# Attention in a decoder block: v's two halves in one product, their sums added once a batch

## The reference

```python
x = x + attn(layernorm(x), w_qkv, w_proj)      # 16 heads of 32, causal softmax, 1.58-bit linear layers
x = x + xattn(layernorm(x), k, skip, ctx, ctx) # long convolution of v*x2 along 512, weighed by x1
x = x + ffn(layernorm(x), gate, up, down, scales)  # silu(gate) * up, weights rounded to fp8
```

```python
attn = einsum('bnhd,bmhd->bhnm', q, k) * SCALE   # masked, then softmax over m
out = einsum('bhnm,bmhd->bnhd', softmax(attn), v).reshape(B, N, C)
return bitlinear(out, w_proj)                    # rounds rows of out by their maximum
```

## Time and profile before

| | us |
|---|---|
| median of 3 runs | 1649.04 (1647.38 to 1649.38) |
| profiled execution | 1647.97 |
| its span | 1646.2 |
| PE busy | 1517.4 (92%) |
| DVE busy | 1280.9 (78%) |
| POOL busy | 974.4 (59%) |
| ACT busy | 676.7 (41%) |
| mean granted TensorE clock | 0.979 |

### The profile page before, as it was taken

How to read it: one execution, slowest core, us unless ns; L and a number is a source line. 1 busy time by engine, 2 the same in 40 slices (tenths; PEclk the granted TensorE clock), 3 DMA queues, 4 the chain that set the end, 5 groups by cost and what they waited for, 6 DMA issues and landing times.

```text
span 1646.2 us, 27188 instructions
## 1 busy us (share of the span) xinstructions
PE 1517.4 (92%) x10581; PEld 869.8 (53%) x10581; DVE 1280.9 (78%) x1865; ACT 676.7 (41%) x1214; POOL 974.4 (59%) x706
## 2 busy tenths in 40 slices
PE   2589999999996778899999999999999999999998
PEld 2477787878774333444444544444444444444443
DVE  5689898998883779888788878877887878778621
ACT  4478788888775101322322322222233222222131
POOL 2278888888874456664655645644654565455242
PEclk9799999999998889999999999999999999999999
DMA  3545464546341513010200120030020020010010
GB/s 131 159 101 143 123 158 117 147 121 156 92 107 69 137 52 96 20 27 1 72 25 7 29 68 7 13 83 8 13 77 13 7 71 26 1 45 0 0 27 26
DMA packets 62048, 105.98 MB, mean 64 GB/s; under 512 B 7880, under 2 KB 14176, under 8 KB 61920
## 3 DMA queue, kind: packets, MB, share of 16 engines
q1 hardware_dynamic: 61728, 104.10, 23.5%
q10 hardware_dynamic: 192, 0.14, 0.1%
HBM read 50.74 MB, written 19.92 MB: 43 GB/s over the span
## 4 chain that ended last, share of the span: by engine, by line
PE 60%; DVE 4%; POOL 2%; issue 1%; POOLq 0%; ACT 0%; DVEq 0%
PE gu L665 20%; PE y L630 10%; PE gu L679 10%; PE y L633 3%; PE y L638 3%; PE y L634 3%; PE gu L618 3%; PE y L637 3%; PE y L636 3%; PE misc L594 1%; PE misc L655 1%; PE misc L645 1%; PE misc L538 1%; DVE z L973 1%; DVE oT L984 1%
## 5 line engine op out<-in xcount | busy, mean ns | idle before, releaser
L1539 POOL TENSOR_TENSOR fuL<-fu,fuH 128x512 f16<-128x512 f32 x96 | 125.2, 1304 | 248.1 <-ACT fuH L1353 248.1
L630 PE MATMUL y<-kv,toep 128*128 128x512 f32 x496 | 241.5, 609 | 21.3 <-DVE z L973 19.0
L1448 POOL TENSOR_TENSOR pL<-pT,pH 128x768 f16<-128x768 f32 x128 | 221.9, 1739 | 28.1 <-ACT pH L1195 20.5
L984 DVE TENSOR_REDUCE oT<-z 128x64 f32<-128x512 f32 x256 | 175.6, 686 | 8.8
L665 PE MATMUL gu<-fT,wg 128*128 128x512 f16 x768 | 181.5, 379 | 0.3 <-ACT fT L1372 0.3
L665 PE MATMUL gu<-fT,wu 128*128 128x512 f16 x768 | 181.5, 379 | 0.0
L980 DVE TENSOR_TENSOR z<-z,cT 128x512 f32<-128x512 f32 x112 | 168.1, 1501 | 3.8
L1353 ACT ACTIVATE fuH<-fu 128x512 f16<-128x512 f32 x96 | 60.2, 627 | 254.7 <-DVE fu L999 254.7
L977 DVE TENSOR_TENSOR z<-y,shared 128x512 f32<-128x512 f32 x112 | 76.8, 686 | 90.9 <-PE y L634 77.0
L1189 ACT ACTIVATE pT<-s_kq,ws 128x768 f32<-128x768 f32 x128 | 115.1, 899 | 78.7 <-PE s_kq L493 53.1
L630 PEld LDWEIGHTS y<-kv,toep 128*128 128x128 f32 x496 | 92.4, 195 | 102.2 <-issue 61.2
(11 more groups left out here) (190 smaller groups left out, 3792.8 us busy)
## 6 DMA issues: line engine op xcount, KB each, us to landing
pack<-qkhl SPq DMA_DIRECT2D x256, 128.0 KB, 2.5
x_sb<-in_x SPq DMA_DIRECT2D x16, 512.0 KB, 5.0
c_sb<-in_ctx SPq DMA_DIRECT2D x32, 256.0 KB, 4.7
hankel<-in_L_xattn_k SPq DMA_DIRECT2D x32, 256.0 KB, 4.3
x_grp<-x_scratch SPq DMA_DIRECT2D x32, 256.0 KB, 3.9
out_y<-yo SPq DMA_DIRECT2D x32, 256.0 KB, 2.9
x_scratch<-x_sb SPq DMA_DIRECT2D x15, 512.0 KB, 3.0
wraw<-in_L_attn_w_qkv SPq DMA_DIRECT2D x3, 1024.0 KB, 9.8
```

Source lines behind the costliest of these rows:

```text
L630: made = T.matmul(to, tap(h, lb - kb), keys_values(h, kb, half), start=kb == 0, stop=kb == lb)
L984: V.tensor_reduce(out=oT[h % 2][:, lb, own].rearrange("p (b j) -> p b j", b=HB), in_=z[n % 2][:], op=ALU.add, axis=AXIS.X).then_inc(m_z, 1)
L1448: G.tensor_tensor(pL[n % 2][:], pT[n % NP][:], pH[n % NP][:], ALU.subtract).then_inc(low_done, 1)
L1539: G.tensor_tensor(fuL[:, ib, :], fu[n % 2][:], fuH[:, ib, :], ALU.subtract).then_inc(f_fl, 1)
```

## The change

- vH and vL become one tile vHL of 65 columns a head: high part (32), ones (1), low part (32). `weigh` multiplies pH and pL by all 65 columns: 12 products a pair. The bank pv then holds, for each head, the sum with v's high part, the row's sum, and apart from them the sum with v's low part: 260 columns, not 132.
- `weighed` copies 260 columns; oraw has 65 a head.
- The two sums are added once a batch: in `finish` k = 0 VectorE does it for the first half of the rows, beside the reciprocal; in the same step GpSimd does it for the second half (`sum_parts`, behind its low part). The multiplication moves to k = 1 and waits for both; the maximum moves to k = 2, VectorE's reciprocal of the step and ScalarE's step to k = 3, ScalarE's rounding of o to k = 4. The transposes stay at k = 5, 6, and all behind them.
- The high part of pair 4 of each batch moves from VectorE to ScalarE (a step 6).
- ScalarE scales a weights' piece in step 5n + 3, not 5n + 5.
- rows_s, a small tile used before the loop, moves to memory that is used again later.

```diff
--- before.py
+++ after.py
@@ -86,7 +86,7 @@
     PIECE = 512
     PIECES = 2 * CB * INNER // PIECE
     NX, NPACK, NP = 8, 3, 3
-    HIGH_ON_ACT = (1, 2, 3, 5, 6, 7)
+    HIGH_ON_ACT = (1, 2, 3, 4, 5, 6, 7)
 
     with ExitStack() as ctx:
         def sb(where, name, shape, dt):
@@ -111,7 +111,6 @@
         cols = sb(ctx, "cols", [P, 2 * IB], F32)
         gs, us = cols[:, 0:IB], cols[:, IB:2 * IB]
         skips = sb(ctx, "skips", [P, M_HEADS, M_POS], F32)
-        rows_s = sb(ctx, "rows_s", [2 * IB, P], F32)
         GROUP = 4
         ws = sb(ctx, "ws", [P, 8], F32)
         stats = sb(ctx, "stats", [P, NT, 6], F32)
@@ -148,14 +147,15 @@
             wraw = [sb(prep, f"wraw{i}", [P, WB, C], F32) for i in range(4)]
             tern = [sb(prep, f"tern{i}", [P, WB, C], BF16) for i in range(2)]
             wsums = sb(prep, "wsums", [P, 4], F32)
+            rows_s = sb(prep, "rows_s", [2 * IB, P], F32)
         packs.append(q("pack2", [P, 2, R, GQ, N], F16))
-        oraw = [q(f"oraw{i}", [P, NT, HEADS, VW], F32) for i in range(2)]
+        oraw = [q(f"oraw{i}", [P, NT, HEADS, VW + D], F32) for i in range(2)]
         fw_raw = [q(f"fw_raw{i}", [P, PIECE], F32) for i in range(3)]
         fw_pow = [q(f"fw_pow{i}", [P, PIECE], F32) for i in range(2)]
         o_sb = q("o_sb", [P, NT, C + 1], F32)
         fw_out = [q(f"fw_out{i}", [P, PIECE], F16) for i in range(2)]
-        vH = [q(f"vH{i}", [P, NT, HEADS, VW], F16) for i in range(3)]
-        vL = [q(f"vL{i}", [P, NT, HEADS, D], F16) for i in range(3)]
+
+        vHL = [q(f"vHL{i}", [P, NT, HEADS, VW + D], F16) for i in range(3)]
         blockmax = [q(f"blockmax{i}", [P, PAIRS, 6], F32) for i in range(2)]
         negmax = [q(f"negmax{i}", [P, NT, 32], F32) for i in range(2)]
         nmT = [q(f"nmT{i}", [P, N], BF16) for i in range(2)]
@@ -248,7 +248,7 @@
         high_act, high_dve, low_done = signal("p_high_act"), signal("p_high_dve"), signal("p_low")
         pv_pe, pv_out = signal("pv_pe"), signal("pv_out")
         o_mult, omax_done, ostep_done, oscale_done = signal("o_mult"), signal("omax"), signal("ostep"), signal("oscale")
-        o_round, c2_done = signal("o_round"), signal("c2")
+        o_sum, o_round, c2_done = signal("o_sum"), signal("o_round"), signal("c2")
         oqT_pe, oqT_done = signal("oqT_pe"), signal("oqT")
         proj_pe, x1_done = signal("proj_pe"), signal("x1")
         fw_in, fw_stored = signals("fw_in", 3), signals("fw_stored", 2)
@@ -495,8 +495,8 @@
 
             def weigh(n):
                 b, p = divmod(n, PAIRS)
-                ph, pl, vh, vl = pH[n % NP], pL[n % 2], vH[b % 3], vL[b % 3]
-                acc = pv[:, 0:NT * 2 * VW].rearrange("p (t h w) -> p t h w", t=NT, h=2)
+                ph, pl, v = pH[n % NP], pL[n % 2], vHL[b % 3]
+                acc = pv[:, 0:NT * 2 * (VW + D)].rearrange("p (t h w) -> p t h w", t=NT, h=2)
                 w.wait_ge(*high_done(n))
                 w.wait_ge(low_done, n + 1)
                 w.wait_ge(v_high, 2 * b + 2)
@@ -507,10 +507,8 @@
                     for hh in range(2):
                         for mt in range(t + 1):
                             block, h = 2 * hh + t if mt == t else 4 + hh, 2 * p + hh
-                            T.matmul(acc[:, t, hh, :], ph[:, block, :], vh[:, mt, h, :], start=mt == 0, stop=False)
-                            T.matmul(acc[:, t, hh, 0:D], ph[:, block, :], vl[:, mt, h, :], start=False, stop=False)
-                            T.matmul(acc[:, t, hh, 0:D], pl[:, block, :], vl[:, mt, h, :], start=False, stop=False)
-                            made = T.matmul(acc[:, t, hh, :], pl[:, block, :], vh[:, mt, h, :], start=False, stop=mt == t)
+                            T.matmul(acc[:, t, hh, :], ph[:, block, :], v[:, mt, h, :], start=mt == 0, stop=False)
+                            made = T.matmul(acc[:, t, hh, :], pl[:, block, :], v[:, mt, h, :], start=False, stop=mt == t)
                 made.then_inc(pv_pe, 1)
 
             def turn_oq(b, j):
@@ -779,11 +777,11 @@
                 w.wait_ge(const_done, C_ONCE)
                 if b >= 3:
                     w.wait_ge(pv_pe, PAIRS * (b - 2))
-                V.tensor_scalar(vH[b % 3][:, t, :, 0:D], bank[:].rearrange("p (h d) -> p h d", h=HEADS),
+                V.tensor_scalar(vHL[b % 3][:, t, :, 0:D], bank[:].rearrange("p (h d) -> p h d", h=HEADS),
                                 small[b % 4][:, 12 + t:13 + t], None, ALU.mult).then_inc(v_high, 1)
                 w.wait_ge(v_high, n + 1)
-                V.scalar_tensor_tensor(out=vL[b % 3][:, t], in0=bank[:].rearrange("p (h d) -> p h d", h=HEADS),
-                                       scalar=small[b % 4][:, 12 + t:13 + t], in1=vH[b % 3][:, t, :, 0:D],
+                V.scalar_tensor_tensor(out=vHL[b % 3][:, t, :, VW:VW + D], in0=bank[:].rearrange("p (h d) -> p h d", h=HEADS),
+                                       scalar=small[b % 4][:, 12 + t:13 + t], in1=vHL[b % 3][:, t, :, 0:D],
                                        op0=ALU.mult, op1=ALU.subtract).then_inc(v_low, 1)
 
             def take_max(n):
@@ -821,18 +819,22 @@
                 rl = osmall[:, 4 * NT:4 * NT + NT * HEADS].rearrange("p (t h) -> p t h", t=NT)
                 if k == 0:
                     w.wait_ge(pv_out, PAIRS * (b + 1))
-                    chain.step(V.reciprocal(rl, oraw[b % 2][:, :, :, D]))
+                    raw = oraw[b % 2]
+                    V.reciprocal(rl, raw[:, :, :, D])
+                    chain.step(V.tensor_tensor(raw[:, 0, :, 0:D], raw[:, 0, :, 0:D], raw[:, 0, :, VW:VW + D], ALU.add))
+                elif k == 1:
                     chain.wait()
+                    w.wait_ge(o_sum, b + 1)
                     if b > 0:
                         w.wait_ge(oqT_pe, 2 * b)
                     V.tensor_tensor(o_sb[:, :, 0:C].rearrange("p t (h d) -> p t h d", d=D), oraw[b % 2][:, :, :, 0:D], rl.unsqueeze(3).broadcast_to([P, NT, HEADS, D]),
                                     ALU.mult).then_inc(o_mult, 1)
-                elif k == 1:
+                elif k == 2:
                     w.wait_ge(o_mult, b + 1)
                     if b >= 2:
                         w.wait_ge(ostep_done, b - 1)
                     V.tensor_reduce(out=am, in_=o_sb[:], op=ALU.max, axis=AXIS.X, apply_absolute_value=True).then_inc(omax_done, 1)
-                elif k == 2:
+                elif k == 3:
                     w.wait_ge(ostep_done, b + 1)
                     V.reciprocal(inv, step).then_inc(oscale_done, 1)
                 elif k in (10, 12):
@@ -1205,12 +1207,12 @@
             def finish(b, k):
                 osmall = osmalls[b % 2]
                 am, step, inv, c2 = (osmall[:, NT * j:NT * (j + 1)] for j in range(4))
-                if k == 2:
+                if k == 3:
                     w.wait_ge(omax_done, b + 1)
                     if b >= 2:
                         w.wait_ge(c2_done, b - 1)
                     S.activation(step, am, ACT.Copy, scale=1.0 / 127.0).then_inc(ostep_done, 1)
-                elif k == 3:
+                elif k == 4:
                     w.wait_ge(oscale_done, b + 1)
                     for t in range(NT):
                         made = S.activation(o_sb[:, t, 0:C], o_sb[:, t, 0:C], ACT.Copy, bias=ROUND, scale=inv[:, t:t + 1])
@@ -1229,7 +1231,7 @@
 
             def weight_pieces(k):
                 n, second = divmod(k - 1, 2)
-                if second and n < PIECES:
+                if not second and n < PIECES:
                     w.wait_ge(fw_pow_done, n + 1)
                     S.activation(fw_pow[n % 2][:], fw_pow[n % 2][:], ACT.Copy, scale=FP8_STEP).then_inc(fw_scaled, 1)
 
@@ -1300,7 +1302,7 @@
                 for use, k in halves(t):
                     if k == 2:
                         high_max(use)
-                if (k := weight_step(t)) is not None and k > 0:
+                if (k := weight_step(t - 2)) is not None and k > 0:
                     weight_pieces(k)
                 if t == PREFETCHED_AT:
                     projected(w)
@@ -1447,6 +1449,11 @@
                     w.wait_ge(pv_pe, n - 1)
                 G.tensor_tensor(pL[n % 2][:], pT[n % NP][:], pH[n % NP][:], ALU.subtract).then_inc(low_done, 1)
 
+            def sum_parts(b):
+                raw = oraw[b % 2]
+                w.wait_ge(pv_out, PAIRS * (b + 1))
+                G.tensor_tensor(raw[:, 1, :, 0:D], raw[:, 1, :, 0:D], raw[:, 1, :, VW:VW + D], ALU.add).then_inc(o_sum, 1)
+
             def weight_pieces(k):
                 if k == 0:
                     return
@@ -1471,10 +1478,12 @@
             for i in range(2):
                 G.memset(nmT[i][:], 0.0).then_inc(const_done, 1)
             for i in range(3):
-                G.memset(vH[i][:, :, :, D:VW], 1.0).then_inc(const_done, 1)
+                G.memset(vHL[i][:, :, :, D:VW], 1.0).then_inc(const_done, 1)
             for t in STEPS:
                 if (n := pair(t, LOW)) is not None:
                     low_part(n)
```

(2 more changed lines are left out.)

## The result

| | before | changed |
|---|---|---|
| median | 1648.76 us (4 runs) | 1638.30 us (4 runs) |
| span of the profiled execution | 1646.2 us | 1635.2 us |
| ratio, 95% interval | | 0.9937 (0.992 to 0.9954) |

The change is a gain of 10.5 us, 0.6%; 1636 was predicted. A second measurement gives 1637.25 beside 1646.96, ratio 0.9946 (0.9934 to 0.9959).

What follows compares the result with a forecast made beforehand. TensorE was taken as the bound, tied in every step to three engines close behind. 0.9 us less a batch, 16 times 14.4, less 1.2 at the end, gave 13.2 us: 1636 us, range 1620 to 1653.

Steps and rivals of the forecast that it cites:

- The products: Attention on TensorE: 12 products of 65 columns a pair, 28 ns apart; 0.27 us less a pair, 2.2 us a batch.
- ScalarE: Wider copy, 0.11 us a pair, and one more high part a batch: together 1.6 us, 23.0 becomes 24.6 a batch.
- VectorE and GpSimd: VectorE loses a cast, gains an addition: 25.2 us a batch; GpSimd gains an addition of 1272 ns: 24.9.
- I give the lost wait no term of its own: GpSimd's 2.9 us a batch of waiting for ScalarE's scaling goes and pays for its addition; no separate gain counted.
- So here the move ... is a gain: Rounding of o on ScalarE leaves full step 0 for step 1 of eight, taking 1.4 us into a step with room.
- The sum: Period 28.2 us a batch would become 26.9 with the same coupling loss; 0.9 us less a batch was taken.
- the forecast: The main case: a gain of 0.7 to 1.3 us a batch in the attention, chance 0.55.
- The new waits: VectorE's multiplication waits for GpSimd's sum; two microseconds cover it in the loop; were they gone, each is paid 16 times.
- The end of the part: After the attention's last batch nothing covers GpSimd's sum: 1.3 us less 0.3, plus latency, +1.2 us once.
- Full gain: Rival: TensorE stays the bound and all 2.2 us a batch come through; 1615 us, or 1620 with VectorE's floor; chance 0.13.
- The slower rival: ScalarE's step 6 grows 0.85 us; if neighbouring steps can't take it up, TensorE idles each batch: 1657 us; chance 0.15.
- second price: In the slower rival, TensorE's idle stretches lower its clock to 1.2 GHz: one or two more falls of about 1.7 us each.

## Why the prediction was right, and where its working was not

The time was: 13.2 us less predicted, 10.5 measured, and 27.3 us a batch forecast, 27.4 measured. The reason it gave for it was not.

- *The products.* 28 ns forecast, 30 measured (the estimate of 29.6 ns by the formula in the Trainium skill's "TensorE: Matmul & The Clock Gate", Back-to-back issue gap, agrees with the profile's 30). TensorE fell to 24.6, forecast 24.3. The size was right, its worth was not: 32 us of it show as 5.4 to 6.9 us.
- *ScalarE.* Copy 375 ns as forecast. 24.1 us a batch, forecast 24.6. But its price was put only into the engine's load, and there it looked harmless (ScalarE the third of four). It was the dearest part of the added work: 8.8 us of 13.
- *VectorE and GpSimd.* Additions of 904 and 1245 ns, forecast 1074 and 1272; 24.8 and 24.7 us a batch, forecast 25.2 and 24.9. They cost 2.4 us together. That they hold each other up is seen at the end of the part, below.
- *"I give the lost wait no term of its own."* This is the step that failed. The wait of 2.9 us a batch of GpSimd, called payment for its addition, is worth 9.2 us by itself, 6.9 of them by the end of the attention. It held the queue of low parts, and these held the exponentials (12.1 us). I had looked only at batches 5 to 13; in the first five of the kernel before GpSimd waited another 23.0 us for the scaling, once 11.9 us at a stretch (waits of 67.6 to 194.7 us):

```profile
POOL fw_raw L1462 <- ACT fw_pow L1234: 23.0, 7, 11.9
```

In the sum a term of 7 to 9 us was missing.
- *"So here the move ... is a gain."* Also wrong. The move of the rounding came with that of multiplication and maximum, and together they cost 6.9 us alone. I had listed that step 7 gets the maximum and gave it no price: step 7 is the one that grew, to 4.34 us.
- *The sum.* The 0.9 us a batch stood for TensorE's 2.2 less what coupling takes back. In truth: 9.2 us from the scaling, 6 from the products, 6 to 8 from pair 4's move where the end of a batch is late, less 6.9 for that late end, 8.8 for the copy, 2.4 for the sums. These were measured in different surroundings and don't add up exactly; their sum is 3 to 6 us, and 10 were measured. The size came out right since a missing gain and missing losses cancelled, which is luck. The chance of 0.55 for the forecast was fair as to the time and not as to its mechanism.
- *The new waits.* Right. VectorE's multiplication never waits for GpSimd's sum in the nine batches: no such row is in the waits. The cover held.
- *The end of the part*, where 1.2 us were forecast. VectorE on the last batch, and GpSimd's addition beside it:

```profile
506.43 0.35 DVE L823 RECIPROCAL osmall<-oraw 128x32 f32<-128x32 f32 x1 [5.36 <-ACT oraw L1205]
506.70 1.39 DVE L824 TENSOR_TENSOR oraw<-oraw 128x512 f32<-128x512 f32 x1
508.12 1.23 DVE L830 TENSOR_TENSOR o_sb<-oraw,osmall 128x1024 f32<-128x1024 f32 x1
...
506.47 1.06 POOL L1455 TENSOR_TENSOR oraw<-oraw 128x512 f32<-128x512 f32 x1 [2.51 <-ACT oraw L1205]
```

From the reciprocal to the multiplication it is 1.69 us, before 0.69 (518.86 to 519.55): 1.0 us more, as VectorE's addition, 1.39 us beside GpSimd's and 0.90 in the mean, stands in the open. GpSimd's ends at 507.53, VectorE's 0.56 us later; VectorE's shortest takes 0.63.
- *The rivals.* Full gain did not come: TensorE is hardly a limit after the change: 6 products fewer a pair brought nothing in the time and 1.8 us in the profile. The slower rival's mechanism, ScalarE's step 6, is real in size (4.45 us, forecast 4.4), but taking 0.4 us out of it brought nothing (with more low clock beside it, so its price stays open); what made TensorE wait was VectorE, 23.1 us in nine batches. Its second price, the clock, is there, but rarely: one low stretch within batches 5 to 13, as before.

## What to carry to other kernels

Where engines are tied to each other in every step, the load of an engine over a batch doesn't price a change: ask at which place of the step the work stands. Here 13 us more of copies on the least loaded engine, which fills some of the steps without a gap, cost two thirds of their length, and 32 us taken off the most loaded one brought a fifth. A wait of a queue on something that could have been made steps earlier was the cheapest gain here, even on an engine that is idle for 16% of the time: price it by what is queued behind it, and test it alone before the large edit.

## What the runs showed of the hardware

Products of 65 columns with a weight load each start 30 ns apart, those of 32 and 33 columns 25 ns, of 128 columns 55 ns. ScalarE's copy from a bank takes 273 ns for 132 and 375 ns for 260 columns.

VectorE and GpSimd hold each other up by whole instructions. In the changed kernel the multiplication of o takes 1.21 to 2.60 us for one shape, and GpSimd's addition 1.07 to 1.53. Two meetings:

```profile
265.35 1.15 POOL L1443 TENSOR_TENSOR qkhl<-qkt,qkhl 128x512 f16<-128x512 f32 x1
265.40 2.19 DVE L830 TENSOR_TENSOR o_sb<-oraw,osmall 128x1024 f32<-128x1024 f32 x1
...
290.68 1.21 DVE L830 TENSOR_TENSOR o_sb<-oraw,osmall 128x1024 f32<-128x1024 f32 x1
290.70 2.21 POOL L1443 TENSOR_TENSOR qkhl<-qkt,qkhl 128x512 f16<-128x512 f32 x1
```

At 265 us GpSimd is first, and VectorE ends 1.09 us after it; at 290 us VectorE is first, and GpSimd ends 1.02 us after it. VectorE's mask over a weights' piece has one input and shows it most plainly. In the kernel before, 22 of its 24 instances start while GpSimd works and end 0.27 to 0.29 us after GpSimd's instruction, whether they take 0.53 us or 1.87; the shortest takes 0.42. VectorE's score reduction, which reads the bank s_qk, doesn't show it: its 128 instances take 0.93 to 0.96 us. So what the mask and the multiplication cost is set by where GpSimd stands when they start, and any edit that moves one of the two engines can change it.
